# A layer kernel on one core: three PSUM banks for the key-major score products and two for the row-maximum products, another order in SyncE's step, and the norm rows made one at a time

## The reference, cut to what matters

```python
def _layernorm(x, axis=-1, eps=1e-05):
    m = jnp.mean(x, axis=axis, keepdims=True)
    v = jnp.var(x, axis=axis, keepdims=True)
    return (x - m) / jnp.sqrt(v + eps)
...
        q = rope(x @ Wq.T)
        k = rope(x @ Wk.T)
        v = x @ Wv.T
        ...
        dot = jnp.einsum('bhqd,bhkd->bhqk', q, k) / jnp.sqrt(jnp.float32(s))
        att = jax.nn.softmax(dot, axis=-1)
        out = jnp.einsum('bhqk,bhkd->bhqd', att, v)
        out = out.transpose(0, 2, 1, 3).reshape(b, t, h * s)
        return out @ Wu.T + bu
...
            xr = mu_r * x + (1.0 - mu_r) * x_prev
            xk = mu_k * x + (1.0 - mu_k) * x_prev
            r = jax.nn.sigmoid(jnp.einsum('btc,dc->btd', xr, W_r))
            k = jnp.einsum('btc,dc->btd', xk, W_k)
            k_act = jnp.square(jax.nn.relu(k))
            out = r * jnp.einsum('btc,dc->btd', k_act, W_v)
...
    x = x + _L0_attn_ref(_layernorm(x, axis=-1), L0_attn_Wq, L0_attn_Wk, L0_attn_Wv, L0_attn_Wu, L0_attn_bu)
    x = x + _L0_ffn_ref(_layernorm(x, axis=-1), L0_ffn_W_r, L0_ffn_W_k, L0_ffn_W_v, L0_ffn_mu_r, L0_ffn_mu_k)
```

## Time and profile before

| | |
|---|---|
| median of 3 runs | 2275.34 us (2271.11 to 2275.67) |
| the profiled execution | 2274.27 us |
| its span in the trace | 2272.4 us, mean granted TensorE clock 0.972 |
| TensorE busy | 2114.4 us, 93% of the span |
| VectorE busy | 1872.0 us, 82% |
| ScalarE busy | 1645.5 us, 72% |
| GpSimd busy | 1514.8 us, 67% |

### The profile page before, as it was taken

One profiled execution on the slowest core, in us unless ns is written; L12 is line 12 of the kernel. 1 busy time (PEld: TensorE's weight loads), 2 busy tenths in 40 slices (PEclk: granted clock), 3 DMA queues, 4 the chain that ended last, 5 costly groups with the idle time before them and its releaser, 6 DMA issues.

```text
span 2272.4 us, 39598 instructions
## 1 busy us (share of the span) xinstructions
PE 2114.4 (93%) x13084; PEld 1085.5 (48%) x13084; DVE 1872.0 (82%) x3598; ACT 1645.5 (72%) x3137; POOL 1514.8 (67%) x1568
## 2 busy tenths in 40 slices
PE   4999999999999999999999999999999999999985
PEld 3445444445454445444444544444445445454433
DVE  5788888878888888888888888888888888888762
ACT  2477777777877777777777777777777777777663
POOL 5347766667866676776676786666777667677335
PEclk8799999999999999999999999999999999999887
DMA  6544455544455553445564445555444556443410
GB/s 153 117 109 106 95 101 120 130 108 106 96 109 111 129 125 99 103 94 110 130 129 110 104 94 110 111 129 120 104 105 95 106 131 130 106 103 88 83 29 23
DMA packets 133467, 242.09 MB, mean 107 GB/s; under 512 B 24849, under 2 KB 79761, under 8 KB 120977
## 3 DMA queue, kind: packets, MB, share of 16 engines
q1 hardware_dynamic: 133264, 239.56, 47.5%
HBM read 136.71 MB, written 83.89 MB: 97 GB/s over the span
## 4 chain that ended last, share of the span: by engine, by line
PE 46%; POOL 18%; issue 15%; ACT 7%; DVE 5%; SPq 5%; DMA 4%; POOLq 0%; ACTq 0%; DVEq 0%
PE d_ps L957 19%; PE st_ps L895 12%; PE pv_ps L927 11%; PE s_ps L913 4%; SPq L314 4%; POOL parts L431 3%; DMA attnT<-attn 3%; DVE mx L707 3%; POOL xrT L440 3%; ACT yn L581 2%; ACT probs L666 2%; POOL f_lo L454 2%; POOL sums L482 2%; POOL rope_t L413 2%; POOL rope_t L416 2%
## 5 line engine op out<-in xcount | busy, mean ns | idle before, releaser
L707 DVE TENSOR_REDUCE mx<-s_ps 128x1 f32<-128x512 f32 x2048 | 1336.6, 678 | 300.9 <-PE s_ps L913 300.5
L666 ACT ACTIVATE probs<-st_ps 128x512 f32<-128x512 f32 x2048 | 1155.7, 597 | 484.9 <-PE st_ps L895 465.5
L895 PE MATMUL st_ps<-q_st,k_st 50*128 50x512 f32 x2048 | 813.3, 461 | 92.3 <-ACT probs L666 50.7
L913 PE MATMUL s_ps<-k_st,q_st 48*128 48x512 f32 x2048 | 815.8, 465 | 7.8 <-DMA k_st<-parts_scratch 5.4
L895 PEld LDWEIGHTS st_ps<-q_st,k_st 50*128 50x128 f32 x2048 | 323.2, 187 | 717.3 <-ACT probs L666 485.1
L927 PE MATMUL pv_ps<-probs,v_ext 128*32 128x512 f32 x4096 | 551.0, 610 | 0.0
L913 PEld LDWEIGHTS s_ps<-k_st,q_st 48*128 48x128 f32 x2048 | 322.6, 187 | 19.1 <-DVE mx L707 10.4
L482 POOL TENSOR_TENSOR sums<-sums,inv 128x256 f32<-128x256 f32 x128 | 93.0, 727 | 305.5 <-DVE inv L734 305.5
L461 POOL TENSOR_TENSOR f_lo<-yn,f_hi 128x512 fp32r<-128x512 f32 x128 | 166.6, 1312 | 44.8 <-ACT f_hi L631 44.7
L927 PEld LDWEIGHTS pv_ps<-probs,v_ext 128*32 128x32 f32 x4096 | 81.1, 108 | 179.1 <-issue 171.3
L431 POOL TENSOR_TENSOR parts<-parts 128x1024 fp32r<-128x1024 f32 x62 | 148.1, 2388 | 19.4 <-ACT parts L596 19.4
(11 more groups left out here) (116 smaller groups left out, 4007.2 us busy)
## 6 DMA issues: line engine op xcount, KB each, us to landing
parts_scratch<-parts SPq DMA_DIRECT2D x64, 1024.0 KB, 4.5
q_st<-parts_scratch SPq DMA_DIRECT2D x128, 256.0 KB, 5.4
k_st<-parts_scratch SPq DMA_DIRECT2D x128, 256.0 KB, 6.3
xn<-in_L_attn_x_dram SPq DMA_DIRECT2D x32, 512.0 KB, 9.2
q_st<-parts_scratch SPq DMA_DIRECT2D x128, 128.0 KB, 6.8
k_st<-parts_scratch SPq DMA_DIRECT2D x128, 128.0 KB, 7.3
attnT<-attn SPq DMA_DIRECT2D x512, 32.0 KB, 2.0
y<-in_L_attn_x_dram SPq DMA_DIRECT2D x32, 512.0 KB, 7.0
```

Of the source, the lines that this page charges most:

```text
L666: nc.scalar.activation(probs[:, u % SLOTS, j, :], st_ps[:, n % 2, :], ACT.Exp, scale=float(D) ** -0.5).then_inc(exp_done, 1)
L707: nc.vector.tensor_reduce(mx[:, col:col + 1], s_ps[:, ring_bank(n), :], AX.X, ALU.max).then_inc(max_done, 1)
L895: nc.tensor.matmul(st_ps[:, n % 2, :], k_st[par][row:row + SROWS + MROWS, slot, c * P:(c + 1) * P], q_st[par][row:row + SROWS + MROWS, slo ...
L913: nc.tensor.matmul(s_ps[:, ring_bank(n), :], q_st[at][row:row + SROWS, slot, qc * P:(qc + 1) * P], k_st[at][row:row + SROWS, slot, :], sta ...
```

## The change

Five things are changed; what is computed stays the same.

1. `st_ps` gets three banks and `s_ps` two. A key-major product now waits for the exponential three places back, a row-maximum product for the maximum two places back. Three weight transposes at the start take another bank accordingly.
2. In SyncE's step `move_max(b, 1)` stands first, ahead of `store_parts` and `move_attn(b-1, 3)`; it stood behind both.
3. The transpose M of group 1 stands ahead of the dense piece V0 in unit 1 (it stood behind), and so its place in `JOBS` is ahead of V0. `split_max` of group 1 follows at (1,1) and (1,2) instead of (1,3) and (2,0).
4. `norm2` is made block by block at (5,3), (6,0), (7,0), (7,2), where two blocks each stood at (6,0) and (7,2); GpSimd's first `scales` of that norm stands ahead of `divide(b, 0)`; VectorE takes the statistics at (5,0), (5,3), (6,0), and the turn of the sums moves from (5,0) to (5,1). `norm1` moves to (15,0), (15,2) of the step before and (0,0), (0,2); its second `scales` stands one piece earlier on GpSimd.
5. Smaller moves on VectorE: the second gate from (0,3) to (0,2), one `shift` from (9,3) to (10,0).

```diff
-        st_ps = ctx.enter_context(nc.psum_tensor("st_ps", [P, 2, T], F32))
-        s_ps = ctx.enter_context(nc.psum_tensor("s_ps", [P, 3, T], F32))
+        st_ps = ctx.enter_context(nc.psum_tensor("st_ps", [P, 3, T], F32))
+        s_ps = ctx.enter_context(nc.psum_tensor("s_ps", [P, 2, T], F32))
...
-        JOBS = [("O", -2, 1, gated, 2, 2), ("V", 1, 0, v_done, 2, 1), ("M", 0, 1, msplit, 8, 4),
+        JOBS = [("O", -2, 1, gated, 2, 2), ("M", 0, 1, msplit, 8, 4), ("V", 1, 0, v_done, 2, 1),
...
-        MAX_T = {1: (0, 1), 5: (0, 2), 9: (0, 3), 13: (1, 0)}
+        MAX_T = {5: (0, 2), 9: (0, 3), 13: (1, 0)}
...
+                move_max(b, 1)
                 store_parts(b.plus(1), 1 - par, 1)
                 move_attn(b.plus(-1), 3)
-                move_max(b, 1)
                 store_out()
                 load_stacks(0)
...
+                scales(b.plus(-1), 0, ln2_stat, ln2_scale, yn_done, mv2, rs2, nm2)
                 divide(b, 0)
-                for n in range(2):
-                    scales(b.plus(-1), n, ln2_stat, ln2_scale, yn_done, mv2, rs2, nm2)
+                scales(b.plus(-1), 1, ln2_stat, ln2_scale, yn_done, mv2, rs2, nm2)
...
-                        for c in (2 * n, 2 * n + 1):
-                            nc.scalar.activation(yn[:, c, :], y[1 - par][:, c, :], ACT.Identity, scale=rs2[:, c:c + 1],
-                                                 bias=nm2[:, c:c + 1]).then_inc(yn_done, 1)
+                        nc.scalar.activation(yn[:, c, :], y[1 - par][:, c, :], ACT.Identity, scale=rs2[:, c:c + 1],
+                                             bias=nm2[:, c:c + 1]).then_inc(yn_done, 1)
...
-                          (6, 0): [(norm2, 0)], (6, 3): [(qk_evac, 0, 0)],
-                          (7, 2): [(norm2, 1)], (7, 3): [(qk_evac, 0, 1)], (8, 2): [(yT_evac, 0)],
+                          (5, 3): [(norm2, 0)], (6, 0): [(norm2, 1)], (6, 3): [(qk_evac, 0, 0)], (7, 0): [(norm2, 2)],
+                          (7, 2): [(norm2, 3)], (7, 3): [(qk_evac, 0, 1)], (8, 2): [(yT_evac, 0)],
...
-                            nc.scalar.activation(probs[:, u % SLOTS, j, :], st_ps[:, n % 2, :], ACT.Exp,
+                            nc.scalar.activation(probs[:, u % SLOTS, j, :], st_ps[:, ring_bank(n), :], ACT.Exp,
...
-                        nc.vector.tensor_reduce(mx[:, col:col + 1], s_ps[:, ring_bank(n), :], AX.X, ALU.max).then_inc(max_done, 1)
+                        nc.vector.tensor_reduce(mx[:, col:col + 1], s_ps[:, n % 2, :], AX.X, ALU.max).then_inc(max_done, 1)
...
-                extras = {(0, 0): [(gate_v, b.plus(-2), 0)], (0, 3): [(gate_v, b.plus(-2), 1)],
+                extras = {(0, 0): [(gate_v, b.plus(-2), 0)], (0, 2): [(gate_v, b.plus(-2), 1)],
                           (1, 0): [(normalise, prev, 3, 0), (normalise, prev, 3, 1)],
-                          (1, 3): [(normalise, prev, 3, 2), (split_max, b, 1, 0)], (2, 0): [(split_max, b, 1, 1)],
+                          (1, 1): [(split_max, b, 1, 0)], (1, 2): [(split_max, b, 1, 1)], (1, 3): [(normalise, prev, 3, 2)],
...
-                    if b.has(SCORES, n - 1):
-                        pe.wait_ge(exp_done, b.count(SCORES, n - 1))
-                    nc.tensor.matmul(st_ps[:, n % 2, :],
+                    if b.has(SCORES, ring_last(n)):
+                        pe.wait_ge(exp_done, b.count(SCORES, ring_last(n)))
+                    nc.tensor.matmul(st_ps[:, ring_bank(n), :],
...
-                    if s.has(SCORES, ring_last(n)):
-                        pe.wait_ge(max_done, s.count(SCORES, ring_last(n)))
-                    nc.tensor.matmul(s_ps[:, ring_bank(n), :], q_st[at][row:row + SROWS, slot, qc * P:(qc + 1) * P],
+                    if s.has(SCORES, n - 1):
+                        pe.wait_ge(max_done, s.count(SCORES, n - 1))
+                    nc.tensor.matmul(s_ps[:, n % 2, :], q_st[at][row:row + SROWS, slot, qc * P:(qc + 1) * P],
...
                         if j == 1:
+                            if u == 1:
+                                row_max_T(b, 1)
                             dense(u, 0)
                             dense(u, 1)
```

More of the change, by code:

```diff
@@ L204, in weight_bank @@
         def weight_bank(w):
-            return (d_ps, st_ps, s_ps)[w // 2][:, w % 2, :] if w < 6 else s_ps[:, 2, :]
+            return (d_ps, st_ps, s_ps)[w // 2][:, w % 2, :] if w < 6 else st_ps[:, 2, :]
         def steps(eng, body, first=FIRST):
@@ L565, in yT_evac, with norm1 @@
                         nc.scalar.activation(ynT[:, n, 1:T + 1], d_ps[:, BANK["YT", n], :], ACT.Copy).then_inc(ynT_done, 1)
-                def norm1(c):
-                    s = b.plus(2)
+                def norm1(s, c):
                     if s.active():
```

20 lines of the change are left out of this document (10 added, 10 removed).

## The result

| | before | after |
|---|---|---|
| median | 2273.23 us (2268.5 to 2275.67, 4 runs) | 2407.21 us (2403.32 to 2413.79, 4 runs) |
| ratio | | 1.0588, 95% interval 1.0564 to 1.0612 |
| profiled execution, span | 2274.27, 2272.4 us | 2406.88, 2405.1 us |
| mean granted clock of TensorE | 0.972 | 0.954 |

The forecast was 2321 us with a range of 2278 to 2352. The direction was right; the loss is 134 us and not 47.

A forecast was written before the change was run, and what follows sets the result against it. TensorE's fixed order was taken to bound the kernel: 62.0 us a step without waits, plus 4.7 (ring) and 1.6 (attention result), made 68.3, 1.5 more than now; 31 x 1.5 = 47 us on 2274.3 gave 2321 us, range 2278 to 2352.

The forecast's parts named there:

- What bounds the kernel: TensorE's fixed order in the repeated step: 66.85 us against 62.0 without waits, so 4.85 us of waits.
- the sum: Repeated step: 62.0 + 6.3 = 68.3 us, 1.5 more than before; 31 x 1.5 = 47 us, giving 2321 us.
- Part 1, the ring: Two banks for row maxima make TensorE wait, mainly at units 1, 6, 8, 10 and 11: 4.7 us a step.
- the floor: TensorE's step without any wait: 14 x 3.92 + 2 x 3.35 + 4 x 0.11 = 62.0 us.
- Part 2, SyncE: Unit 4: the attention result's DMAs start 1.85 us later, so TensorE waits 1.6 us a step for WU0.
- Parts 3 to 5: Norm statistics and scales come earlier; ScalarE's 31.0 us wait and TensorE's waits behind it go; splitting costs nothing.
- The clock rival: All TensorE products: more short pauses lower the granted clock to 0.95, another 100 us, 2420 us; chance 0.03.
- The upper case: Repeated step: waits at their upper end, 5.3 + 2.0 = 7.3 us, step 69.3, 2350 us; chance 0.2.

The follow-up runs named there:

- experiment 1: The changed kernel with SyncE's order of before (store_parts, move_attn, move_max), all else changed: 2345.05 us, 1.0306 of before.
- experiment 3: The changed kernel with the row-maximum product s(4,1) issued eight more times ahead of st(4,1), filling TensorE's pause: 2377.76 us, 1.0460 of before.
- experiment 6: The kernel before with only the norm parts (part 4 of the change): 2248.94 us, 0.9892 of before.
- experiments 7 and 8: The changed kernel with the banks and SyncE's order of before: 2288.88 us; the same with gate and shift also put back where they were: 2260.51 us.
- experiment 2: The changed kernel with the banks of before (two for st_ps, three for s_ps), all else changed: 2339.03 us, 1.0283 of before.
- experiment 4: The kernel before with only the banks changed (three for key-major products, two for row maxima): 2337.56 us, 1.0276 of before.

## Why the prediction was right in sign and wrong in size

- *What bounds the kernel.* Right: TensorE's own order; the repeated step gives 133 of the 134 us. But the loss is waits and a lower clock behind one of them, and the sum had waits alone.
- *Part 1, the ring, 4.7 us a step.* The mechanism and its places were right; the term was mis-sized. Without its 0.3 for unit 4 it was 4.4 for the units outside XT and WU0. In experiment 1 these lie 69.11 - 62.0 - (4.65 - 3.35) - (4.07 - 3.92) = 5.6 us above the floor. Units 8, 10 and 11 came as forecast: YT +0.6, K0 and K1 +1.1 each, against 0.5, 1.1, 1.1. Unit 6 (WU1) is 1.3 and not 0.9, and the units from R0 to V0 are 1.4 together where I had 0.8. 1.2 us a step were missing, 37 us. I had read three of these places from rows and put the rest together at 0.3.
- *Part 2, SyncE, 1.6 us a step.* This is the step that failed: "So it waits 1.6 us for WU0", for GpSimd's `f_lo`, with the clock's loss at nothing. XT and WU0 are 5.76 + 5.30, 3.8 us above the ones without waits, 0.3 of which stood in part 1, and TensorE waited for other things. I named what hangs on the attention result, `high_a`, `low_a` and WU0, but not what is queued behind `high_a` on ScalarE: two exponentials and `xnT_hi`. With them TensorE is held at pair 1 of unit 4, where the sum had it arrive on time. The lateness itself was nearly right (1.85 us forecast; ScalarE's wait at that place grew by 1.5 on average, from 0.9 to 2.4). Of the 1.9 us a step that were missing, the clock is about 1 (experiment 3: WU0 5.30 to 4.17, 1.1 by the step and 29 us by the medians), and the wait handed on by ScalarE the rest.
- *Parts 3 to 5.* ScalarE's wait for `nm` went as said. The norm parts alone on before are worth 24 us (experiment 6). The moved shift was costed only as VectorE's delay; what ScalarE's `high_f` and GpSimd's low part lose by it did not stand in the sum. With the old banks it is part of 28 us (experiments 7 and 8, the gate moved with it). In the changed kernel TensorE waits for that `f_lo` hardly at all (8.2 us in 4 times); it is held by the ring in units 10 and 11 before that. That the shift costs nothing there is argued from this row and not shown by a run.
- *The clock rival* had the right cause under the wrong conditions. It was priced as a clock of 0.95 for all products, from many short pauses, with a chance of 0.03. What happened is one stretch of 3.7 us in a step at 0.56 behind two waits that lie together, 1.73 + 0.71 = 2.4 us. The window of the earlier trace rows did not bear on it: the wait that stands for it there is 1.14 us. What did bear on it are the two steps of before with a slow WU0, which neither the four steps nor the window that I read hold. By the rule of the Trainium skill (TensorE: Matmul & The Clock Gate, "A second HAM failure mode: psum-queue depth-cycling") the cycling through PSUM banks would be what makes the clock swing. The traces disagree as to the cause here: with the ring's waits and without the late attention result (experiment 1) the clock from 1000 to 1200 us is 1.00, and without the ring (experiment 2) WU0 is slow in 11 of 12 steps. In experiment 4, the ring alone, the clock falls at WU0 in 5 of 12 steps, where before has 2; there the ring has a part in it, as it seems by way of a longer pause for `mparts`.
- *The sum.* 62.0 + 5.6 + 3.8 = 71.4 against the measured 71.37 and the forecast 68.3. Of the 3.1 missing, 1.2 is the ring and 1.9 the attention result with its clock. 31 x 3.1 = 96 us, where 87 were missing: the forecast also counted from a step of 66.85 us, read from four steps, and the mean of 12 in before is 67.09. The upper case (7.3 us of waits) stopped short because its bounds, too, left ScalarE's queue and the clock behind a pause out.
